# Two gated cross-attention layers on one core: counting the key and value stores apart, and another order of loads and of small work in the context stages

## The reference

```
x = x + tanh(g_xattn[0]) * quantised(layernorm(x)) @ quantised(ctx)      # 8-bit fake quantisation
x = x + tanh(g_ffn[0])  * (layernorm(x) @ W_base.T + b + low-rank update through an inverse rfft)
x = x + tanh(g_xattn[1]) * attention(layernorm(x), keys and values of [ctx, layernorm(x)])   # 16 heads, 4 kv heads of 96
x = x + tanh(g_ffn[1])  * (flat * w_sum + top-8 mix of expert biases)
```

## Time and profile before

| what | us |
|---|---|
| median of 3 runs | 1095.9 |
| lowest and highest | 1095.38 and 1097.76 |
| profiled execution, its own time | 1099.59 |
| its span in the trace | 1097.7 |
| PE busy in it | 1043.4 (95%) |
| DVE, ACT, POOL busy | 618.7, 620.1, 644.9 |

### The profile page before, as it was taken

How to read it: one execution, slowest core, us unless ns; L and a number is a source line. 1 busy time by engine, 2 the same in 40 slices (tenths; PEclk the granted TensorE clock), 3 DMA queues, 4 the chain that set the end, 5 groups by cost and what they waited for, 6 DMA issues and landing times.

```text
span 1097.7 us, 18325 instructions
## 1 busy us (share of the span) xinstructions
PE 1043.4 (95%) x7207; PEld 586.4 (53%) x7207; DVE 618.7 (56%) x1067; ACT 620.1 (56%) x687; POOL 644.9 (59%) x349
## 2 busy tenths in 40 slices
PE   8969999999999989999999999999999999989875
PEld 3535544444544555556566655656655655655542
DVE  6866949653223455545545554654654654666656
ACT  5656635432123577656666755656755566667733
POOL 4358678332000588656668845667865567677841
PEclk9979999999999999999999999999999999989996
DMA  9777664753223999999999999999999999999993
GB/s 339 251 233 210 203 221 125 163 96 58 70 92 102 199 205 207 202 207 183 198 179 212 198 198 185 182 201 197 189 206 199 173 209 180 165 168 179 181 170 115
DMA packets 522281, 198.94 MB, mean 181 GB/s; under 512 B 487684, under 2 KB 502916, under 8 KB 522196
## 3 DMA queue, kind: packets, MB, share of 16 engines
q1 hardware_dynamic: 522196, 197.78, 87.2%
HBM read 56.88 MB, written 13.63 MB: 64 GB/s over the span
## 4 chain that ended last, share of the span: by engine, by line
PE 77%; SPq 7%; DMA 6%; DVE 4%; POOL 2%; ACT 2%; issue 1%; POOLq 0%; DVEq 0%; ACTq 0%
PE ps L560 30%; PE ps L796 17%; PE ps L770 9%; PE ps L811 9%; PE ps L813 5%; DMA region_o<-region_y 3%; PE ps L697 3%; SPq L522 2%; SPq L520 2%; POOL region_y L1699 2%; PE ps L582 2%; DMA v_scratch<-region_o 1%; SPq L499 1%; DVE p_max L1535 1%; DMA region_c<-region_b 1%
## 5 line engine op out<-in xcount | busy, mean ns | idle before, releaser
L1699 POOL TENSOR_TENSOR region_y<-p,region_b 128x1536 f16<-128x1536 f32 x128 | 396.9, 3101 | 287.6 <-ACT region_b L1238 225.4
L1535 DVE TENSOR_REDUCE p_max<-ps 128x1 f32<-128x1536 f32 x128 | 224.9, 1757 | 130.5 <-PE ps L796 130.5
L1228 ACT ACTIVATE p<-ps,p_max 128x1536 f32<-128x1536 f32 x128 | 197.0, 1539 | 172.9 <-DVE p_max L1535 172.9
L796 PE MATMUL ps<-region_q,region_c 96*128 96x512 f16 x1152 | 270.1, 379 | 0.8 <-DMA region_c<-region_q 0.8
L1238 ACT ACTIVATE region_b<-ps,p_max 128x1536 f16<-128x1536 f32 x128 | 196.6, 1536 | 66.0 <-DMA region_c<-region_b 66.0
L811 PE MATMUL ps<-region_q,region_c 128*128 128x192 f16 x1536 | 209.1, 247 | 16.5 <-DMA region_o<-region_y 11.9
L813 PE MATMUL ps<-region_q,region_o 128*128 128x96 f16 x1536 | 203.8, 207 | 0.0
L811 PEld LDWEIGHTS ps<-region_q,region_c 128*128 128x128 f16 x1536 | 150.7, 98 | 37.9 <-issue 18.5
L796 PEld LDWEIGHTS ps<-region_q,region_c 96*128 96x128 f16 x1152 | 105.4, 98 | 109.0 <-issue 1.4
L813 PEld LDWEIGHTS ps<-region_q,region_o 128*128 128x128 f16 x1536 | 150.8, 98 | 12.2 <-issue 0.3
L560 PE MATMUL ps<-region_w,region_q 128*128 128x512 f16 x576 | 136.0, 382 | 3.9 <-POOL region_w L1699 2.4
(11 more groups left out here) (147 smaller groups left out, 1108.4 us busy)
## 6 DMA issues: line engine op xcount, KB each, us to landing
stage<-ctx_in SPq DMA_DIRECT2D x16, 512.0 KB, 4.9
stage<-ctx_t_in SPq DMA_DIRECT2D x15, 512.0 KB, 7.4
stage<-wq_in SPq DMA_DIRECT2D x16, 384.0 KB, 4.1
stage<-wo_in SPq DMA_DIRECT2D x16, 384.0 KB, 4.4
k_scratch<-region_o SPq DMA_DIRECT2D x12, 384.0 KB, 5.8
region_q<-k_scratch SPq DMA_DIRECT2D x8, 576.0 KB, 5.8
region_q<-v_scratch SPq DMA_DIRECT2D x8, 576.0 KB, 6.5
x_res<-x_in SPq DMA_DIRECT2D x8, 512.0 KB, 10.0
```

What stands on the lines that cost most here:

```text
L796: ins = nc.tensor.matmul(bank(NSB * (m % 2) + sb_), q_head[0:HD, b, h, hq, qt * P:(qt + 1) * P], k_head[0:HD, b, hk, sb_ * 512:(sb_ + 1) * ...
L1228: nc.scalar.activation(p32[:, m % 2, :], rows, ACT.Exp, bias=p_max[:, m % 4:m % 4 + 1], accum_out=den[:, m % 4:m % 4 + 1]).then_inc(e32_ok, 1)
L1535: nc.vector.reduce_max(p_max[:, m % 4:m % 4 + 1], rows, axis=AX, negate=True).then_inc(max_ok, 1)
L1699: return nc.gpsimd.tensor_tensor(out, a, b, op)
```

## The change

The two key stores and the value store of a piece get functions and semaphores of their own (`k_stored`, `v_stored`). ScalarE waits for `k_stored` before `keys(t)` and for `v_stored` before the first value tile of a piece. On SP the stores, the x tile loads, the turned x tiles and the two encoder loads stand elsewhere among the context loads. On ScalarE and VectorE two places of the program are reordered: `scale_x(3)` behind `values(1, 1)`, and `values(1, 1)` ahead of `stats(4)`, with `quant_x(3)` behind `stats(5)`.

```
-            def store_kv(t, b, s0):
+            def store_keys(t, b, s0):
                 sp.wait_ge(k_lo_ok, NJ * (t + 1))
...
+                    sp.dma_start(dst, k_out[:, :, h, :]).then_inc(k_stored, 16)
+
+            def store_values(t, b, s0):
                 sp.wait_ge(v_lo_ok, 4 * (t + 1))
...
+                sp.dma_start(dst, v_out[:, :, :, :]).then_inc(v_stored, 16)
...
             for n in range(RING):
                 load_ctx(0, n)
+            store_keys(0, 0, 0)
             turn_x(0)
             turn_x(1)
+            load_ctx(0, 4)
+            store_values(0, 0, 0)
+            for n in range(RING + 1, NC):
+                load_ctx(0, n)
+            turn_x(2)
             for n in range(RING, NC):
-                load_ctx(0, n)
                 load_x(n)
-            store_kv(0, 0, 0)
+            load_ctx_t(2, n_done, RING + 1)
+            store_keys(1, 0, QL)
+            turn_x(3)
+            load_ctx_t(3, c_split, 2 * RING + 1)
+            store_values(1, 0, QL)
             sp.wait_ge(low_zero, 2)
             sp.dma_start(enc_f[0:R, :], enc_d).then_inc(enc_ld, 16)
             sp.dma_start(enc_f[R2:RK, :], enc_d).then_inc(enc_ld, 16)
-            turn_x(2)
-            load_ctx_t(2, n_done, RING + 1)
-            turn_x(3)
-            load_ctx_t(3, c_split, 2 * RING + 1)
-            store_kv(1, 0, QL)
             turn_x(4)
...
             def keys(t):
                 if t > 0:
-                    act.wait_ge(kv_stored, 48 * t)
+                    act.wait_ge(k_stored, 32 * t)
...
             def values(t, tt):
                 act.wait_ge(v_ready, 4 * t + tt + 1)
+                if t > 0 and tt == 0:
+                    act.wait_ge(v_stored, 16 * min(t, 4))
...
             keys(1)
-            scale_x(3)
             values(1, 0)
             add_beta(0)
             add_beta(1)
             values(1, 1)
+            scale_x(3)
             split_ctx(2, (0, 1))
...
             keys(1)
-            quant_x(3)
             values(1, 0)
+            values(1, 1)
             dve.wait_ge(x_ld, 2 * 16 * TPB)
             stats(4, LN1)
             stats(5, LN1)
-            values(1, 1)
+            quant_x(3)
             stats(6, LN1)
             stats(7, LN1)
             values(1, 2)
```

More of the change, by code:

```diff
@@ L190, in flamingo @@
         v_ready, v_hi_ok, v_lo_ok = sem("v_ready"), sem("v_hi_ok"), sem("v_lo_ok")
-        kv_stored = sem("kv_stored")
+        k_stored, v_stored = sem("k_stored"), sem("v_stored")
         bn_step, bn_go, ln_var, ln_pow, ln_ok = sem("bn_step"), sem("bn_go"), sem("ln_var"), sem("ln_pow"), sem("ln_ok")
@@ L348, in store_kv, with store_values @@
                     dst = k_dram[b, h].rearrange("(j p) s -> p j s", p=P)[:, :, s0:s0 + QL]
-                    sp.dma_start(dst, k_out[:, :, h, :]).then_inc(kv_stored, 16)
+                    sp.dma_start(dst, k_out[:, :, h, :]).then_inc(k_stored, 16)
+            def store_values(t, b, s0):
                 sp.wait_ge(v_lo_ok, 4 * (t + 1))
                 dst = v_dram[b].rearrange("k p s w -> p k s w")[:, :, s0 // P:s0 // P + 4, :]
-                sp.dma_start(dst, v_out[:, :, :, :]).then_inc(kv_stored, 16)
+                sp.dma_start(dst, v_out[:, :, :, :]).then_inc(v_stored, 16)
             def store_k(b):
@@ L401, in _ @@
             sp.dma_start(enc_f[R2:RK, :], enc_d).then_inc(enc_ld, 16)
[L402 to L406, removed]
             turn_x(4)
@@ L412, in _ @@
                 load_ctx(1, n)
-            store_kv(2, 1, 0)
+            store_keys(2, 1, 0)
+            store_values(2, 1, 0)
             for n in range(RING):
@@ L419, in _ @@
                 load_ft(n, f_used, n - RING + 1)
-            store_kv(3, 1, QL)
+            store_keys(3, 1, QL)
+            store_values(3, 1, QL)
             for n in range(NC):
```

## The result

The changed kernel takes 1092.3 us in the median (five runs, four of them 1090.4 to 1094.4), the kernel before on the same chip 1097.3 (1095.4 to 1098.1). The ratio is 0.9942, interval 0.9915 to 0.9968: 3.5 to 9.3 us faster (the two medians differ by 5.0), where 10.9 us were forecast and 1082.2 to 1090.3 given as the range. A second measurement of the same kernel (label after_again) gave 1091.8 against 1098.6, ratio 0.9933.

A forecast was written before the change was run, and what follows sets the result against it. TensorE was taken as the bound, stalled 10.1 us for VectorE's region_o, with a slowed clock. A ceiling of 12.9 us less 1.7 and 0.3 gave 10.9 off 1095.9, thus 1085.0 us; range 1082.2 to 1090.3.

The forecast's parts named there:

- The ceiling: TensorE's 10.11 us wait in piece 1's values plus 2.95 of slow clock; project_k(2) could start 12.9 us earlier.
- steps 1 to 3: Early stores, context piece 7 and project_k(2)'s context: the old wait goes whole, project_k(2) starts at 69.56, new waits 0.
- Step 4, the first wait: VectorE's queue ends values(2, 0) at 94.3, TensorE wants it at 93.1: a wait of 1.2 us.
- Step 4, the second wait: Two context quantisations on VectorE, the first under GpSimd, put values(2, 1) at 98.8: 0.5 us late.
- step 2: Before piece 1's third value tile: TensorE's wait taken as 0, bound 1.1 us, a size not costing the clock.
- small slacks: Rounding of the slacks of steps 2 and 3: 0.3 us taken off the gain.
- A: The forecast case: 9 to 12.3 us gained, 1083.6 to 1087 us; chance 0.48.
- Step 5: ctx_t loads of piece 3 behind turn_x(3): context split at 80 to 81, wanted at 85.3, cost nothing.
- Step 6: From piece 2's end on: order as before, so the offset stays; no gap from the Fourier product until attention.
- The multiply: VectorE's coef multiply, kept at 1.15 us; by the page possibly 2.50, the wait growing 1.35 and the gain 9.6.
- C: Larger new wait from late x tiles, VectorE or project_k(2)'s context: about 1089.5 us, from 1087 to 1092; chance 0.22.

The follow-up runs named there:

- both moves: Changed kernel with the coef multiply and row sum earlier on VectorE and values(2, 1) ahead of two context quantisations; 1085.4 us against 1098.6 for the kernel before.
- no_sums: Changed kernel with GpSimd's four sums of context chunks 4 to 7 cut to 8 of 1024 columns; 1088.3 us against 1097.8 for the kernel before.
- coef_early: Changed kernel with VectorE's coef multiply and row sum moved from behind values(1, 2) to behind quant_ctx(0, 4); 1091.0 us against 1098.6 for the kernel before.
- old_engine_order: Changed kernel with scale_x(3), quant_x(3) and values(1, 1) back at their old places on ScalarE and VectorE; 1092.7 us against 1097.8 for the kernel before.
- one_count: Changed kernel with all three stores counted on one semaphore again, waited for at the head of keys(t); 1091.9 us against 1097.8 for the kernel before.
- x_between: Changed kernel with loads of x tiles 4 to 7 back between the first batch entry's context tiles; 1094.9 us against 1097.6 for the kernel before.

## Why the prediction was wrong, and where it was right

**The ceiling and steps 1 to 3 held.** Of the 12.9 us both moves together gave back 12.55. No wait for `v_scratch` is left, the value stores land in 4.4 to 6.7 us. I had `values(1, 0)` at 60.6 and it came at about 60.8 (VectorE's x4 from 58.48 on 2.34 us); context piece 7 was scaled at about 55.8, forecast 55.5; project_k(2) at 69.56, measured 69.81; `turn_x(3)` at 70.5, measured 71.39.

**Step 4, the first wait, held.** The sum of the queue was 94.3, measured 94.3; the wait 1.2, measured 1.07. That it fits to the tenth is in part luck: the text has 6.1 us for each of the three x quantisations, the sum 5.7, 6.0 and 6.1, and they took 6.0, 6.5 and 5.1. The contention with GpSimd that it rests on is shown by no_sums for the context quantisations. For those of x, coef_early has the same two instructions at 0.69 and 0.70 us while GpSimd had only one-column work:

```profile
77.36 0.69 DVE L1353 TENSOR_SCALAR region_y<-region_y 128x1024 f32<-128x1024 f32 x1
78.08 0.70 DVE L1357 TENSOR_SCALAR region_s<-region_y 128x1024 f16<-128x1024 f32 x1
```

In the changed kernel they took 2.50 and 2.50 beside a split, from 79.61 on.

**Step 4, the second wait, is the step that failed.** I had "`values(2, 1)` at 98.8, 0.5 us late again" and it was done at 101.2, a wait of 2.79 us. The mechanism was named, its size was off. I let GpSimd end at 96, so that only the clip of the first context quantisation would run beside it. GpSimd ended at 98.85, so the round paid as well. Half of these 2.85 us is length: four splits took 9.74 and four sums 9.71, where I had 9 and 9 and the kernel before took 9.29 and 9.16. The other half is a start at 79.44 instead of 78. Two one-column instructions of GpSimd, 0.55 us in their other places here, took 0.99 beside a round and 1.53 beside the coef multiply:

```profile
70.77 0.99 POOL L1709 TENSOR_TENSOR rstd<-var_c,mhalf 128x1 f32<-128x1 f32 x1
76.93 1.53 POOL L1709 TENSOR_TENSOR rstd<-var_c,mhalf 128x1 f32<-128x1 f32 x1
```

The second one took 0.55 us at the same 76.93 in coef_early, where the multiply was gone from there. The cost of contention was laid on VectorE only, and GpSimd pays it too. The term is 2.3 us short.

**The clock was left out.** It is the second step that failed: the sum puts the clock's cost behind the new waits at nothing. The sentence of step 2, that a wait of that size doesn't cost the clock, holds for one wait (coef_early: 2.57 us, clock 1.00). The two waits of 1.07 and 2.79 us with one tile between them cost 5.75 - 3.94 = 1.8 us. Over the stage the change gained 7.25 us instead of 10.9. The 3.65 missing are 2.3 and 1.8, less 0.1 for the first wait and less the 0.3 taken for small slacks that no wait in the trace claims. At the cross product it is 6.8, because this execution began the stage 0.5 us later. The bound of 6 us in step 4 held this, but the forecast of A took its low side.

**The rest of the miss is not the change.** The median that I took the gain off, 1095.9, was low: with more runs it was 1097.3 to 1098.6. And the stretch from the Q product to the end, the same work in every version, took 772.0 us in the profiled execution before, 773.2 after, 769.4 in after_again and 773.7 in no_sums. A difference of medians of one set of runs has this in it, so the gain is read better over the stage (7.3) and from the repeated ratio (0.9933).

**Step 5 held**, TensorE never waited for `region_c`. **Step 6** held for the changed kernel in that no new wait follows up to the Q product. The place it gives as 126.7 instead of 137.5, once as the Fourier product and once as the third tile of piece 3, is the start of the Fourier product: 137.37 before and 130.61 after. The third tile came at 142.72 and 135.96. And in the faster versions the column sums of GpSimd come 0.4 to 0.7 us late at 138 to 140, which I had not foreseen.

**The multiply.** The Trainium skill, page GPSIMD Engine Reference, section Key points, has instructions with two SBUF inputs contend as well. In the changed kernel the coef multiply took 1.15 us and met no split; there GpSimd paid, as the 1.53 us above show, and the growth of 1.35 us that the prediction worked out did not come on VectorE. In old_engine_order it began in the middle of a split and took twice as long:

```profile
75.74 2.34 DVE L1412 TENSOR_TENSOR region_q<-region_q 128x960 f32<-128x960 f32 x1
```

So the traces agree with the page that the two contend. In these three cases the one that began second was the one that took longer: the multiply here (the next split behind it was late too, the pair took 5.14 us), the one-column instruction in the changed kernel, and in the kernel before the pair of splits that began 0.5 us behind the multiply (4.72 us, 4.21 for the pair before it), with the multiply at 1.15.

**Of the rivals**, C came nearest in kind (VectorE 3 us behind, the clock down again): the gain of 6.8 us at the cross product (7.3 over the stage) lies in its band of 4 to 9, the median of 1092.3 just above its 1092. The chance of it, 0.22, was low for a walk in which GpSimd's end was not worked out with the same care as VectorE's.

## What to carry to other kernels

When an instruction queue is compressed by taking a stall out, work out both queues that share a resource, each with the stretch that the other gives it; the end of the slower one decides how many instructions pay. A wait shown with one cause can have several causes of nearly the same lateness behind it: here, with the store out of the way, the context tile let `keys(1)` start only 2.7 us sooner and the x quantisation took 3.7 us longer, so that moving the store alone won nothing (ratio 1.0009). The result of an engine that the bottleneck waits for goes ahead of work that no one waits for yet: one moved line, `values(2, 1)`, took 5.5 us off the changed kernel, about as much as the whole change had (5.0 to 6.9 by the medians).

## What the runs showed of the hardware that was not expected

A clip or a round of 128x1024 takes 0.69 us alone and mostly 2.5 to 2.6 beside GpSimd's tensor operations, and a multiply with two SBUF inputs 1.15 and 2.34. GpSimd pays as well: four sums took 9.71 us, for 9.16 in the kernel before, and a one-column instruction 1.53 us for 0.55. TensorE's clock stayed at 2.4 GHz over one wait of 2.57 us and one of 2.43, and was lowered after waits of 1.07 and 2.79 us with a tile of 4 us between them, in both executions of the changed kernel, in one_count and, with 1.33 and 2.80, in x_between. No run separates the nearness of the two waits from their sum of 3.9 us.
